# A two-part setup and a second feed-forward matrix in 16-bit halves, in a fused convolution, attention and feed-forward kernel

## The reference, cut to what matters

```
h = group_norm(x, 32 groups);  q, k, v = qkv_w @ h + b          # 1x1 convolution
x = x + proj_w @ (v @ softmax(q.T k / sqrt(128)).T) + proj_b    # attention over all 1024 positions
t = tokens(x)
a = layer_norm(t)                                               # windows of 32 tokens, 8 heads of 16
y = layer_norm1(a + out_w @ window_attention(a) + out_b)
t = t + layer_norm2(y + w2 @ relu(w1 @ y + b1) + b2)            # 128 -> 512 -> 128
t = t + (fp8(layer_norm(t)) @ fp8(kernel) + bias)               # values rounded to 8 bits, then multiplied
```

## Time and profile before

| | us |
|---|---|
| three runs | 2457.88, 2459.72, 2463.32; median 2459.72 |
| the profiled execution | 2464.32 |
| its span | 2462.6 |
| TensorE busy | 2184.8 (89%), 21489 matmul records |
| VectorE busy | 1878.0 (76%) |
| ScalarE busy | 1380.6 (56%) |
| GpSimd busy | 1224.1 (50%) |

### The profile page before, as it was taken

How to read it: one execution, slowest core, us unless ns; L and a number is a source line. 1 busy time by engine, 2 the same in 40 slices (tenths; PEclk the granted TensorE clock), 3 DMA queues, 4 the chain that set the end, 5 groups by cost and what they waited for, 6 DMA issues and landing times.

```text
span 2462.6 us, 63216 instructions
## 1 busy us (share of the span) xinstructions
PE 2184.8 (89%) x21489; PEld 1606.4 (65%) x21710; DVE 1878.0 (76%) x5861; ACT 1380.6 (56%) x2721; POOL 1224.1 (50%) x1303
## 2 busy tenths in 40 slices
PE   1798899999999999999999999999999999999984
PEld 0566667766667766666776666676666677666663
DVE  5488777778777778887777888777887777788753
ACT  0355566555565555556655556665555655555653
POOL 5044455544455645455554545555544555444544
PEclk9999999999999999999999999999999999999997
DMA  1011111111101111110111111111111011111110
GB/s 34 14 31 44 43 28 38 26 38 43 43 26 39 27 40 38 43 43 26 38 26 40 41 43 38 30 38 26 38 43 43 26 38 26 41 40 43 29 31 19
DMA packets 76238, 86.15 MB, mean 35 GB/s; under 512 B 20640, under 2 KB 55584, under 8 KB 76192
## 3 DMA queue, kind: packets, MB, share of 16 engines
q1 hardware_dynamic: 62512, 52.51, 9.3%
q10 hardware_dynamic: 13680, 33.04, 3.9%
HBM read 18.36 MB, written 16.78 MB: 14 GB/s over the span
## 4 chain that ended last, share of the span: by engine, by line
PE 63%; DVE 11%; issue 6%; ACT 4%; DMA 4%; SPq 1%; ACTq 1%; POOL 1%; DVEq 0%; POOLq 0%
PE ps L944 16%; PE ps L851 9%; PE ps L852 8%; PE ps L853 8%; PE ps L1037 6%; PE ps L1006 5%; DMA x_sb<-in_x 3%; PE ps L911 3%; PE ps L988 3%; PE ps L954 2%; PE ps L927 2%; DVE cm L682 2%; DVE stats L723 1%; DVE y L794 1%; ACT o_sb L573 1%
## 5 line engine op out<-in xcount | busy, mean ns | idle before, releaser
L382 POOL TENSOR_TENSOR rstd<-veps,halfpow 128x4 f32<-128x4 f32 x256 | 266.7, 1042 | 816.0 <-DVE veps L731 814.9
L944 PEld LDWEIGHTS ps<-vg,p 128*128 128x128 f32 x4096 | 511.1, 192 | 49.0 <-issue 12.1
L944 PE MATMUL ps<-vg,p 128*128 128x129 f32 x4096 | 533.2, 277 | 0.6 <-ACT p L508 0.6
L508 ACT ACTIVATE p<-ps 128x512 f32<-128x512 f32 x512 | 294.4, 587 | 260.6 <-PE ps L853 260.6
L682 DVE TENSOR_REDUCE cm<-ps 128x1 f32<-128x512 f32 x512 | 330.4, 676 | 16.9 <-PE ps L911 16.7
L1037 PEld LDWEIGHTS ps<-w,hid 128*128 128x128 f32 x2048 | 235.2, 192 | 17.9 <-ACT hid L560 12.8
L1037 PE MATMUL ps<-w,hid 128*128 128x128 f32 x2048 | 242.3, 277 | 1.8 <-ACT hid L560 1.7
L851 PE MATMUL ps<-qgh,kgh 128*128 128x512 f16 x512 | 194.5, 380 | 42.9 <-DVE shift L700 19.9
L911 PE MATMUL ps<-kgh,qgh 128*128 128x512 f16 x512 | 173.9, 392 | 61.5 <-ACT vg L501 37.4
L560 ACT ACTIVATE hid<-ps,cols 128x512 f32<-128x512 f32 x256 | 170.7, 686 | 72.3 <-PE ps L853 72.3
L853 PE MATMUL ps<-qgh,kgl 128*128 128x512 f16 x512 | 194.5, 380 | 0.0
(11 more groups left out here) (188 smaller groups left out, 5439.9 us busy)
## 6 DMA issues: line engine op xcount, KB each, us to landing
ptbd<-et SPq DMA_DIRECT2D x512, 64.0 KB, 2.0
kbd<-kk SPq DMA_DIRECT2D x512, 32.0 KB, 2.0
out_y<-o_sb ACTq DMA_DIRECT2D x64, 256.0 KB, 2.3
x_sb<-in_x ACTq DMA_DIRECT2D x31, 512.0 KB, 3.3
x_sb<-in_x SPq DMA_DIRECT2D x1, 512.0 KB, 3.5
e<-in_w_t SPq DMA_DIRECT2D x1, 256.0 KB, 3.6
w<-in_w_t SPq DMA_DIRECT2D x1, 256.0 KB, 3.4
xt<-in_in_w_t SPq DMA_DIRECT2D x1, 192.0 KB, 2.8
```

The lines of the kernel that those rows point to most:

```text
L382: g.tensor_tensor(rstd[:, k, h, :], veps[:, k, h, :], halfpow[:], ALU.pow).then_inc(s[f"ln_pow{k}"], 1)
L508: sc.activation(p32[:, c % PRING, :], bank("st", c), ACT.Exp, scale=C ** -0.5).then_inc(s["p_made"], 1)
L944: last = mm(ps[:, b, at:at + PVW], p32[:, c % PRING, part], vg32[:, j, :], start=j == 0 and q % 2 == 0, stop=j == MT - 1, skip_group_check ...
```

## The change

Several things change together, and the order of all engines is written anew.

- **`down`**: `w2` is split in the setup into `w2h` and `w2l`. `up` on ScalarE writes the activation twice, `fh` (fp16) and `hid` (32 bits), and GpSimd writes `fl` = `hid` - `fh`. `down` is `three` for each of 4 x 4 tiles: 48 products of 128 columns a half.
- **The shift**: `cparts` becomes bf16 and its transpose with it; ScalarE copies 8 rows of it to `shift`; `st` has four products of 128 columns with `sel` (now -1 at two rows) in place of one of 512.
- **`turn_x`** moves from VectorE to ScalarE, which also adds the bias to the image in place (`bias_x`, once an image).
- **The setup**: seven loads besides the image signal `first_in`; the chain ahead of the first projection has 7 links, and 31 more run in `setup_rest`, on VectorE behind `maxima:0` of image 0 and on TensorE behind `shift:0`. GpSimd zeroes `v32`, `kbd` and `ptbd` in 2, 16 and 8 pieces.
- The output is written from `z` instead of a tile of its own.

```diff
@@ -45,33 +45,34 @@
 PV_BANKS = (6, 7)
 PROGRAM = {
     "pe": """
-        max:1@0- vg:1@5- max:2@4- max:3@3- pv0:0@1-- max:4@2- max:5@4- turn_in:1@0-- pv1:0-- max:6@5- max:7@3-
-        k:1@0-- out:0@4-- v:1@5-- max:8@0- q:1@3-- turn_x:0@2- shift:0@4- max:9@1- max:10@5- st:0@0- max:11@1-
-        turn_mid:0@3-- pv:0- score0:1@4-- score1:1@2-- up0:0@0-- st:1@5- st:2@1- up1:0@3-- turn_x:1@4- max:12@5-
-        up2:0@2-- up3:0@3-- pv:1- max:13@0- down:0@2-- st:3@0- max:14@3- max:15@5- pv0:1@1-- pv1:1-- pv:2- st:4@0-
-        out:1@2-- st:5@5- st:6@0- pv:3- pv:4- gn1:0@0 shift:1@3- st:7@1- pv:5- turn_mid:1@3-- pv:6- pv:7- up0:1@2--
-        up1:1@1-- up2:1@0-- up3:1@4-- st:8@3- down:1@5-- st:9@2- st:10@5- turn_in:0@2- pv:8- st:11@3- k:0@0- pv:9-
-        st:12@2- q:0@1- pv:10- st:13@3- pv:11- st:14@2- gn2:0@3 turn_q:0@5-- st:15@3- pv:12- pv:13- score0:0@1-
-        score1:0@0- v:0@2- pv:14- qg:0@4 kg:0@5 pv:15- vg:0@0 turn_q:1@2-- kg:1@3 qg:1@1 ffn:0@5-- max:0@5 ffn:1@2--""",
+        max:5@0- k:1@3-- pv1:0-- max:6@1- max:7@3- out:0@4-- q:1@1-- vg:1@0- max:8@5- max:9@4- v:1@3-- shift:0@3-
+        st:0@5- score0:1@3-- turn_mid:0@4-- score1:1@2-- st:1@1- up0:0@0-- max:10@5- up1:0@1-- up2:0@3-- max:11@0-
+        pv:0- st:2@2- up3:0@1-- max:12@3- max:13@5- st:3@0- pv:1- pv0:1@1-- max:14@3- max:15@2- down:0@4--
+        turn_x:0@0- pv1:1-- turn_x:1@4- st:4@3- out:1@2-- st:5@0- pv:2- st:6@5- pv:3- st:7@1- shift:1@5- pv:4-
+        turn_mid:1@4-- pv:5- pv:6- up0:1@3-- pv:7- up1:1@0-- st:8@4- up2:1@3-- up3:1@5-- st:9@0- pv:8- st:10@4-
+        pv:9- down:1@5-- st:11@4- gn1:0@5 turn_in:0@0- k:0@0- pv:10- pv:11- st:12@4- q:0@2- gn2:0@3 turn_q:0@0--
+        st:13@5- st:14@1- ffn:0@5-- pv:12- pv:13- st:15@4- score0:0@0- score1:0@1- pv:14- pv:15- vg:0@4 kg:0@5
+        turn_q:1@3-- qg:0@4 kg:1@1 v:0@0- ffn:1@3-- max:0@0 qg:1@2 max:1@3 max:2@5 max:3@0 turn_in:1@3- max:4@5
+        pv0:0@4-""",
     "dve": """
-        prob1:0-- kg:0- pv:15-- turn_p0:0-- ln_in:1-- qg:0- turn_p1:0-- max:0- kg:1- qg:1- max:1- max:2- max:3-
-        max:4- max:5- turn_in:1-- max:6- pv1:0-- max:7- k:1-- out:0-- maxima:0- max:8- shift:0- max:9- q:1--
-        turn_x:0- max:10- max:11- turn_mid:0-- score0:1-- score1:1-- prob0:1-- prob1:1-- turn_p0:1-- turn_x:1-
-        turn_p1:1-- gn0:0 max:12- max:13- down:0-- max:14- max:15- pv1:1-- out:1-- maxima:1- shift:1- gn1:0
-        turn_mid:1-- ln_q:0-- pv:7- ln_in:0- quant:0-- down:1-- turn_in:0- k:0- ln_q:1-- q:0- gn2:0 quant:1--
-        score0:0- score1:0- prob0:0-""",
+        prob1:0-- pv:15-- turn_p0:0-- ln_in:1-- turn_p1:0-- kg:0- qg:0- max:0- max:1- max:2- max:3- turn_in:1--
+        kg:1- max:4- max:5- k:1-- pv1:0-- max:6- max:7- out:0-- maxima:0- max:8- q:1-- qg:1- max:9- score0:1--
+        turn_mid:0-- prob0:1-- score1:1-- turn_p0:1-- max:10- max:11- prob1:1-- max:12- max:13- turn_p1:1-- max:14-
+        max:15- down:0-- pv1:1-- maxima:1- out:1-- turn_mid:1-- ln_q:0-- gn0:0 pv:7- ln_in:0- quant:0-- down:1--
+        turn_in:0- gn1:0 k:0- ln_q:1-- q:0- gn2:0 quant:1-- score0:0- score1:0- prob0:0-""",
     "act": """
-        vg:1- turn_in:1-- pv1:0-- k:1-- q:1-- v:1-- norm_mid:0-- st:0- turn_mid:0-- score0:1-- up0:0-- st:1-
-        score1:1-- st:2- up1:0-- load_x:0 up2:0-- up3:0-- st:3- pv1:1-- st:4- norm_out:0-- st:5- st:6- norm_mid:1--
-        st:7- turn_mid:1-- up0:1-- up1:1-- up2:1-- up3:1-- quant:0-- st:8- norm_in:0- st:9- turn_in:0- st:10-
-        norm_out:1-- k:0- st:11- q:0- st:12- st:13- quant:1-- gn2:0 st:14- st:15- turn_q:0-- v:0- score0:0-
-        score1:0- kg:0 turn_q:1-- qg:0 ffn:0-- qg:1 kg:1 vg:0 ffn:1-- norm_in:1-""",
+        pv1:0-- qg:1- q:1-- vg:1- v:1-- shift:0- norm_mid:0-- turn_mid:0-- st:0- score0:1-- st:1- up0:0-- up1:0--
+        up2:0-- score1:1-- up3:0-- st:2- st:3- turn_x:0- pv1:1-- st:4- norm_out:0-- st:5- turn_x:1- st:6-
+        norm_mid:1-- turn_mid:1-- load_x:0 shift:1- st:7- up0:1-- up1:1-- st:8- up2:1-- up3:1-- st:9- quant:0--
+        st:10- norm_in:0- st:11- turn_in:0- norm_out:1-- k:0- st:12- turn_q:0-- st:13- q:0- ffn:0-- quant:1-- gn2:0
+        st:14- bias_x:0 st:15- score0:0- score1:0- vg:0 kg:0 qg:0 turn_q:1-- kg:1 v:0- ffn:1-- norm_in:1- turn_in:1-
+        k:1-""",
     "pool": """
-        prob1:0-- ln_in:1-- out:0-- norm_mid:0-- prob0:1-- prob1:1-- bias_out:1-- keep:0-- down:0-- out:1--
-        norm_out:0-- norm_mid:1-- ln_q:0-- keep:1-- ln_in:0- quant:0-- down:1-- norm_out:1-- ln_q:1-- gn2:0
-        quant:1-- prob0:0- bias_out:0-""",
+        bias_out:0-- bias_out:1-- keep:0-- out:0-- prob0:1-- up0:0-- up1:0-- up2:0-- prob1:1-- up3:0-- norm_mid:0--
+        down:0-- keep:1-- out:1-- norm_out:0-- norm_mid:1-- ln_q:0-- up0:1-- up1:1-- up2:1-- up3:1-- ln_in:0-
+        quant:0-- down:1-- norm_out:1-- ln_q:1-- gn2:0 quant:1-- prob0:0- prob1:0- ln_in:1-""",
     "sp": """
-        k:0-- place0:0-- place1:0-- k:1-- place0:1-- place1:1--""",
+        place0:0- place1:0- k:1- place0:1- place1:1- k:0""",
 }
...
-        w2 = sb("w2", [P, FT, P])
+        w2h, w2l = sb("w2h", [P, FT, P], F16), sb("w2l", [P, FT, P], BF16)
...
-        sel = sb("sel", [2 * HT, HT, P])
-        minus1 = sb("minus1", [P, P], BF16)
+        sel = sb("sel", [P, HT, P], BF16)
...
+        fh, fl = sb("fh", [P, FT, HALF], F16), sb("fl", [P, FT, HALF], F16)
...
+                load(wraw[:, QG:QG + 2, :].rearrange("p a b -> p (a b)"), a["qkv_w_t"][:, 0:2 * P], "first_in")
+                load(wraw[:, VG, :], a["v_w"], "first_in")
+                load(wraw[:, PROJ, :], a["proj_w_t"], "first_in")
                 with nc.allow_non_contiguous_dma("short vectors, once"):
-                    for at, width, name in ((QGB, 3, "qkv_b"), (PROJB, 1, "proj_b"), (GNW, 1, "gn_w"), (GNB, 1, "gn_b"),
-                                            (QB, 3, "in_b"), (LN1B, 1, "ln1_b"), (FFNB, 1, "ffn_b"), (B1, FT, "b1"),
+                    for at, width, name in ((QGB, 3, "qkv_b"), (GNW, 1, "gn_w"), (GNB, 1, "gn_b"), (PROJB, 1, "proj_b")):
+                        load(cols[:, at:at + width], a[name].rearrange("(t p) -> p t", p=P), "first_in")
+                    load(wraw[:, Q:Q + 3, :].rearrange("p a b -> p (a b)"), a["in_w_t"])
...
-                for tile in (v32, kbd, ptbd):
-                    g.memset(tile[:], 0.0).then_inc(s["const_made"], 1)
+                for h in range(2):
+                    g.memset(v32[:, h], 0.0).then_inc(s["const_made"], 1)
+                    for head in range(HEADS):
+                        g.memset(kbd[:, h, head], 0.0).then_inc(s["const_made"], 1)
+                    for j in range(HT):
+                        g.memset(ptbd[:, h, j], 0.0).then_inc(s["const_made"], 1)
...
+            def up(f):
+                def step(kind, img, h):
+                    n = 2 * img + h
+                    pool.wait_ge(s["hid_made"], upto(n, f + 1, per=FT))
+
+                    if due(value := upto(n - 1)):
+                        pool.wait_ge(s["down_mm"], value)
+                    g.tensor_tensor(fl[:, f, :], hid[:, f, :], fh[:, f, :], ALU.subtract).then_inc(s["hid_lo"], 1)
...
+            def bias_x(kind, img, _):
+                act.wait_ge(s["h32_made"], upto(img))
+                if isinstance(img, int) and img == 0:
+                    act.wait_ge(s["setup_dve"], SETUP_FIRST)
+                sc.activation(x_sb[:], x_sb[:], ACT.Identity, bias=col(PROJB)).then_inc(s["x_bias"], 1)
+
+            def turn_x(kind, img, c):
+                act.wait_ge(s["turn_x_mm"], upto(img, c + 1, per=2))
+
+                if due(value := upto(2 * img + c - 2)):
+                    act.wait_ge(s["t_made"], value)
+                sc.activation(xt[:, c], tiles(bank("turn_x", c)), ACT.Copy).then_inc(s["xt_made"], 1)
...
+            def make_shift(kind, img, c):
+                act.wait_ge(s["shift_turned"], upto(img, c + 1, per=2))
+                sc.activation(shift[0:2 * HT, c, :], bank("shift", c)[0:2 * HT, 0:P // 2].bitcast(BF16),
+                              ACT.Copy).then_inc(s["shift_made"], 1)
...
+                    sc.activation(fh[:, f, :], bank(f"up{f}", h), ACT.Relu, bias=col(B1F + f)).then_inc(s["hid_hi"], 1)
...
-                dve.wait_ge(s["weights_in"], 16 * 26)
-                dve.wait_ge(s["const_made"], 10)
-                dve.wait_ge(s["const_mask"], 6)
-                link(v_.tensor_scalar(vb_full[:, 0, :], ones, col(VGB), None, ALU.mult))
-                link(v_.tensor_scalar(vb_full[:, 1, :], ones, col(VB), None, ALU.mult))
                 gn1(None, 0, 0)
+                dve.wait_ge(s["first_in"], 16 * 7)
+                halves(QG)
+                halves(KG)
                 gn2(None, 0, 0)
                 dve.wait_ge(s["setup_mm"], 1)
-                for w in (QG, KG, Q, K, V, OUT):
-                    link(v_.tensor_copy(wh[:, w, :], wraw[:, w, :]))
-                    link(v_.tensor_tensor(wl[:, w, :], wraw[:, w, :], wh[:, w, :], ALU.subtract))
                 link(v_.tensor_copy(wh[:, PVG, :], ps[:, 6, 0:P]))
```

(68 more changed lines are left out.)

86 lines of the change are left out of this document (46 added, 40 removed).

## The result

The changed kernel is slower: 2690.7 us (median; 2682.7 to 2694.2) against 2460.1, a ratio of 1.093 [1.090, 1.096]. The forecast was 2419, so it missed by 272 us, and on the wrong side.

A forecast was written before the change was run, and what follows sets the result against it. VectorE (near stretch) and TensorE (rest) were taken to bound by turns. From 2464.3: setup −43.7 and +10.5, periods −9.3, drain +2, median −4.6, giving 2419 us; own range 2389 to 2449, with 8 in 10 2375 to 2449.

The forecast's parts named there:

- the period of 72.1: Steady image period: near stretch 24.9 plus rest 46.8 plus 0.4 for other waits, 0.3 us less than now.
- First projection at 15.1 instead of 58.8: Setup: fewer loads and links ahead of the first projection let it start 43.7 us earlier.
- A gap of about 10 near 30 to 42: First image: sign expected in TensorE's work, about 10 us, while VectorE runs the late setup steps.
- Given back +10.5: Setup behind shift:0: VectorE's late steps delay the queued max steps; 10.5 us of the gain lost, between 6 and 15.
- rival C: Setup behind shift:0 costs more: every cast held, clock falls, first image ends late; +20 us, 2439; chance 0.10.
- A cast is held for under 0.9 and not for 15: Setup: GpSimd's zeroing in 26 pieces of at most 0.86 us limits how long each VectorE cast is held.
- down at 2.72: TensorE: 48 16-bit products of 57 ns a half; saves 0.84 us a half, 1.7 an image.
- Near stretch: Period from score0:0's end to up0:0's start, bound by VectorE's unbroken row; at least 24.9 us, was 27.05.
- Rest 46.8: Period's remainder, TensorE's: 45.35 us before, 46.8 after, with moved steps and 1.97 of new waits.
- The old cover of k:0: TensorE: other steps once filled the 1.64 us between turn_in and k; the new order loses that.
- Rival B: GpSimd's queue ahead of down:1 late by 2.8 us a period; +87 us, 2506; chance 0.12.
- Rival A: TensorE bounds the kernel all through, so its 1.5 us an image arrives whole; 2381 or 2360 us; chance 0.18.

The follow-up runs named there:

- e9: The changed kernel with 22 extra 32-bit products of one column (88 instructions) in TensorE's setup, ahead of the loop; 2505.4 us, 1.018.
- e3: The kernel before with the two-part setup alone; order, down and shift as before; 2435.7 us, 0.990.
- e12: e3 with the late setup links in nine pieces, behind maxima:0, shift:0 and max:9 to max:15, instead of one queue; 2432.5 us, 0.987.
- e1: The changed kernel with TensorE's 28 steady iterations written out, no loop there; other engines keep theirs; 2523.8 us, 1.027.
- e4: The changed kernel with down back in 32 bits, without fh, fl and GpSimd's subtractions; 2552.3 us, 1.039.
- e10: e9 with TensorE's k:0 two steps later, behind pv:10 and pv:11; 2473.3 us, 1.005.
- e18: e10 with down:1 ahead of pv:9 and GpSimd's last two subtractions of half 1 cut to 8 columns; 2456.7 us, 0.999.
- e6: e3 with down as three 16-bit products and GpSimd's subtractions, in the old order but for down:1, two steps later; 2731.2 us, 1.109.
- e5: e2 with 64 extra products of 128 columns once in the setup, ahead of the loop; 2467.0 us, 1.003.
- e2: The kernel before with the shift product of st split in four, 96 more instructions in TensorE's loop; 2595.6 us, 1.057.
- e8: The kernel before with TensorE's iterations written out instead of looped; 2507.7 us, 1.018.

## Why the prediction was wrong

**The step that failed is the period of 72.1.** It was built from what engines do and wait for, and had no term for TensorE's own instructions. The change gives TensorE 169 more of them an iteration (1483 to 1652), and I counted them as time (57 ns each), never as room. Where the body came to lie, each jump back fetched nine blocks: 4.3 us of standing, some 4 us at a clock of 0.53 to 0.68 behind it, 7.1 a period (82.15 against 75.05) and 185 us in all by e9. The prediction named no such rival, and its bounds for the period (71.3 to 73.1) could not hold it. A second part failed as well: without the fetch the period is 75.05, still above the 73.2 that the prediction named as its sign of being wrong.

Term by term:

- *First projection at 15.1 instead of 58.8*: 13.38. Right, and 1.7 better.
- *A gap of about 10 near 30 to 42*: in the changed kernel TensorE stands for 14.1 us up to 40.73, for cm, while VectorE goes through its queue.
- *Given back +10.5, setup −33*: e3 has −23, so the give-back is some 12 us larger. That is rival C's direction at half of its price. "A cast is held for under 0.9 and not for 15" is what failed: one was held for 10.25. That it comes from the queue behind maxima:0, as I put it, is only partly so (e12).
- *down at 2.72*: right. In e1 its 48 products run from 1179.06 to 1181.74, where the next step starts, 2.68. The saving arrives whole, too, 1.7 to 1.8 a period in the new order (e4 and e9).
- *Near stretch at least 24.9, VectorE without pause*: 26.1 without the fetch (e9). VectorE is busy for 24.4 in it, so my count of its steps (24.5) was right, and its pauses, 1.7 where I allowed 0.4, were not: it waits for TensorE and ScalarE too.
- *Rest 46.8, of it 1.64 for k:0 right behind turn_in:0*: 49.4 in the period of e9 that is shown. The waits were right: 1.6 for xl (8.0 us in five periods) and 0.2 for ol, 1.85 in all against 1.97. TensorE's busy time was not: 47.5 against the 44.8 that is left of 46.8. Of these 2.7 us 1.6 are gone in e10, whose rest has a clock of 1.00 where e9's has 0.97; the sum had no term for the clock, which fell behind this wait in 9 of e9's 26 steady periods. Another 0.7 was a misreading: the sum took 0.73 off as TensorE's own waits in the old rest, and these were matmul records missing from that trace. e3, the same order with all 679 records of a period (the kernel before has 671, and what is missing is the shift product of `st`), stands for 0.05 there:

```profile
1219.11:1264.40 45.29, 45.24 (x389) 33.52 (x388) 31.94 (x117) 27.21 (x54) 24.68 (x29) 1.00 0.11 29
```

- *TensorE busy for 65.7*: 67.9 in e10. One microsecond of the 2.2 is those missing records (67.2 in the kernel before, 68.2 in e3); the rest wasn't settled.
- *The other engines at 55, 51 and 47*: VectorE 55.2, ScalarE 50.6, GpSimd 46.1. Right.
- *The old cover of k:0*: filling the wait of k:0 gave 1.1 a period (e10) of its 1.6, since the chain from down:1 through norm_out:1, kk and the keys' DMAs crosses the stretch that I had called TensorE's, and two other waits came up.
- *Rival B*: GpSimd ahead of down:1. Its mechanism is there, at 0.4 us a period in the new order (e18) in place of 2.8, and at 2.5 a period in the old (e6). The power's spread, by which I priced it, isn't what does it: the subtractions are (1.16 us each, inside my 1.06 to 1.27).
- *Rival A*, TensorE as the bound all through with a period of 70.9, is excluded by e9 and e10, although `down`'s part of its saving did arrive whole.
- *The range*: its upper end was added up wrong. 2464.3 − 28 + 22 + 2 − 4.6 is 2456, not 2449; the measured time is far outside either.

The sum of the 272 missed: 185 are the fetch (the changed kernel against e9), and 86 lie between e9 and the forecast. Of these, the 27 later periods are 66 (2.46 a period more than e3's) where the forecast had −8, so 74; the setup is 10 (e3). The first four periods of e9 are 10 shorter than e3's and its drain is 8 longer, 6 more than forecast, which leaves some 6 open. Each of the two losses alone would have turned the direction: e9, without the fetch, is still 1.8% slower than the kernel before.

## What to carry to other kernels

Before a change adds instructions to a long loop, count the instructions of the body as well as their time, and look at the packets of the instruction queue: if they grow with the iterations, the loop fetches itself again, and some instructions ahead of it can take that away (88 and 128 here). When a saving lies on one engine, follow each moved step through the in-order queues of the others up to the next DMA, since a sum over two chains misses the third. Look at the granted clock of single periods as well: two orders with equal periods at full clock differed by 13 us. Of this change, the setup gained 23 us and `down` in halves 47; the new order of the engines, with the steps that it moves, lost more than both (4.2 a period, e4 against e3).

## What the runs showed of the hardware

- A loop body of 1579 TensorE instructions ran without fetching at one place (e5), and stalled at 16 of 27 jumps 128 instructions earlier (e2); one of 1652 at none or every jump, 88 apart (e9, after).
- After 4.3 us of standing TensorE came back at a granted clock of 0.53, 1.2 GHz instead of 2.4, and was at 1.00 again within 5 us. In e9 it was 0.71 and 0.87 in the two windows of 4 us at and behind a wait of 1.6 us, and the same wait left it at 1.00 in 17 of 26 periods.
- Written out, the kernel before is 1.8% slower than in its loop (e8), with longer waits for the DMAs of ptbd and kbd while q8 moves 181 packets instead of 28.
- A cast of four columns on VectorE took 10.25 us and ended with the last of 26 back-to-back memsets of GpSimd (e3); in other executions it got in between two of them (0.39, the changed kernel).
